# Routed expert blocks with two PSUM banks each for turned tokens and finished blocks, tokens turned two ahead, and lists built from 64 rows and 32 marks

## What is computed

```python
# E, F, K = 16 experts, 128 hidden units, 2 choices; 2 shared experts
y = gelu(x @ g[e] + gb[e]) * (x @ w1[e] + b1[e]);  out = y @ w2[e] + b2[e]
aff = sigmoid(x @ wa);  p, i = top_k(aff, 2);  p = p / sum(p)
routed = sum over the 2 chosen experts of p * expert(x)
shared = sum over the 2 shared experts of expert(x)
x = x + (x + shared + routed)     # on the layer-normed x within the brackets
```

## Time and profile before

| | us |
|---|---|
| median of 3 runs | 969.54 |
| lowest and highest | 968.85, 970.51 |
| the profiled execution, time of the run | 969.79 |
| the profiled execution, span in the profile | 968.5 |
| busy: PE, DVE, ACT, POOL | 879.2, 717.4, 596.9, 589.9 |
| layer 0: first `turn_in` to last `turn_out` | 604.21 to 667.47 |
| layer 1: first `turn_in` to last `turn_out` | 890.05 to 951.22 |

### The profile page before, as it was taken

How to read it: one execution, slowest core, us unless ns; L and a number is a source line. 1 busy time by engine, 2 the same in 40 slices (tenths; PEclk the granted TensorE clock), 3 DMA queues, 4 the chain that set the end, 5 groups by cost and what they waited for, 6 DMA issues and landing times.

```text
span 968.5 us, 23186 instructions
## 1 busy us (share of the span) xinstructions
PE 879.2 (91%) x9330; PEld 731.1 (75%) x9330; DVE 717.4 (74%) x1287; ACT 596.9 (62%) x970; POOL 589.9 (61%) x603
## 2 busy tenths in 40 slices
PE   8799999999999999999999898899689888888992
PEld 6578788878888888888788886788566447676981
DVE  4788889788888987897888758643594877357744
ACT  4888877787787687777876541453497345241551
POOL 4895698678677876886786844423338641332342
PEclk9999999999999999999999999999899899899997
DMA  4321212021112111121110393963012112462644
GB/s 124 112 76 65 73 45 88 34 77 56 65 56 78 45 67 56 45 88 34 44 56 2 96 259 115 312 230 132 11 44 68 22 30 55 131 172 94 237 153 164
DMA packets 68417, 89.79 MB, mean 93 GB/s; under 512 B 11570, under 2 KB 49494, under 8 KB 68310
## 3 DMA queue, kind: packets, MB, share of 16 engines
q1 hardware_dynamic: 63062, 77.81, 25.1%
q0 software_dynamic: 3072, 8.39, 2.8%
q10 hardware_dynamic: 2176, 2.10, 0.6%
HBM read 59.57 MB, written 8.52 MB: 70 GB/s over the span
## 4 chain that ended last, share of the span: by engine, by line
PE 57%; DVE 24%; POOL 5%; ACT 5%; issue 5%; DMA 2%; another core or an unknown queue 0%; ACTq 0%; DVEq 0%; POOLq 0%; SPq 0%
PE psum L826 21%; DVE arena L1945 7%; PE psum L1125 5%; PE psum L798 5%; PE psum L909 4%; PE psum L901 4%; PE psum L954 3%; PE psum L1139 2%; DVE arena L1982 2%; PE psum L1263 1%; DVE v L2378 1%; PE psum L1297 1%; PE psum L1227 1%; DVE arena L2001 1%; DMA arena<-scratch_y 1%
## 5 line engine op out<-in xcount | busy, mean ns | idle before, releaser
L826 PE MATMUL psum<-vT,split 128*128 128x512 f32 x1368 | 343.1, 400 | 7.9 <-DVE arena L1945 5.5
L1945 DVE SCALAR_TENSOR_TENSOR arena<-psum,arena 128x1023 f32<-128x1023 f32 (+2 forms) x208 | 265.7, 1278 | 74.0 <-ACT arena L1454 51.4
L826 PEld LDWEIGHTS psum<-vT,split 128*128 128x128 f32 x1368 | 248.8, 188 | 63.6 <-DVE arena L1945 7.6
L1454 ACT ACTIVATE arena<-psum,arena 128x512 f32<-128x512 f32 x160 | 109.1, 690 | 66.2 <-PE psum L826 65.6
L1471 ACT ACTIVATE arena<-arena 128x1024 f32<-128x1024 f32 x80 | 84.2, 1058 | 34.9 <-POOL arena L2557 23.3
L2530 POOL TENSOR_TENSOR split<-arena,split 128x256 fp32r<-128x256 f32 x114 | 83.6, 742 | 30.7 <-ACT split L1381 30.6
L2557 POOL TENSOR_TENSOR arena<-arena,v 128x1021 f32<-128x1021 f32 x32 | 76.3, 2386 | 41.8 <-DVE arena L1945 41.8
L798 PE MATMUL psum<-ident,arena 128*128 128x128 f32 x568 | 73.0, 274 | 9.8 <-POOL arena L2587 6.1
L798 PEld LDWEIGHTS psum<-ident,arena 128*128 128x128 f32 x568 | 63.9, 140 | 21.3 <-POOL arena L2587 9.7
L1125 PE MATMUL psum<-arena,vT 128*128 x496 | 67.0, 278 | 3.4 <-issue 1.9
L1125 PEld LDWEIGHTS psum<-arena,vT 128*128 128x128 f32 x496 | 60.3, 192 | 6.5 <-issue 6.3
(11 more groups left out here) (283 smaller groups left out, 1733.9 us busy)
## 6 DMA issues: line engine op xcount, KB each, us to landing
bcast<-scratch_a SPq DMA_DIRECT2D x32, 512.0 KB, 3.7
vT<-arena SPq DMA_DIRECT2D x62, 256.0 KB
arena<-in_w_a SPq DMA_DIRECT2D x16, 768.0 KB, 4.2
arena<-in_wout_a SPq DMA_DIRECT2D x8, 256.0 KB, 2.6
scratch_v<-v SPq DMA_DIRECT2D x8, 256.0 KB, 5.2
arena<-scratch_y ACTq DMA_DIRECT2D x8, 256.0 KB, 5.2
arena<-scratch_y SPq DMA_DIRECT2D x8, 256.0 KB, 5.3
arena<-in_wg SPq DMA_DIRECT2D x4, 512.0 KB, 5.9
```

Of the source, the lines that this page charges most:

```text
L826: m = pe.matmul(bank, split[:, t % SPLITS, i, q, :], vT[:, j, q, half * BANK:(half + 1) * BANK], start=(n == 0), stop=(n == 3 * KD - 1))
L1454: act.activation(tile[:, hs], wide_of(t)[:, hs], ACT.Identity, scale=w[:, TAPS - 1:TAPS], bias=0.0).then_inc(sem["tap0"], 1)
L1945: dve.scalar_tensor_tensor(out=tile[:, s:T], in0=bank[:, 0:T - s], scalar=cw_a[:, j, i, TAPS - 1 - s:TAPS - s], in1=tile[:, s:T], op0=ALU. ...
```

## The change

`in_bank` becomes two banks (2 and 4) and `out_bank` two (1 and 5), used in turn. `turn_in(i)` waits for `block_in(i - 2)` and `block_down(j)` for `block_out(j - 2)`. Banks 4 and 5 hold shared sums, so `turn_in(1)` waits for `add_shared(0)` and `block_down(1)` for `add_shared(1)`; these two move from steps 5 and 6 to before the first blocks on DVE, ahead of `add_v` of the same tokens. `turned_after(j)` is j + 2 for all j, with `turn_in(1)` ahead of `block_up(0)`. In a step PE does `block_down(j - 1)` before `turn_out(j - 17)`, and DVE `block_in(j + 2)` before `block_hidden(j)`.

The list's base is now a multiple of 64 (`SUB`): 32 marks to a list, 64 rows, a table `halves` for the 32 bases, one DVE instruction for all of `hot`, and 32 matmuls in `members` that give 64 partitions each. `members` stands ahead of both parts of `up(3)`.

```diff
 def turned_after(j):
-    return [1] if j == 0 else [2, 3] if j == 1 else [j + 2] if j + 2 < DENSE else []
+    return [j + 2] if j + 2 < DENSE else []
...
-ADD_SHARED_AT = (5, 6, 7, 8)
+ADD_SHARED_AT = (None, None, 7, 8)
...
-        out_bank, in_bank, row_bank = (psum[:, i * BANK:i * BANK + D] for i in (1, 2, 2))
+        out_banks, in_banks = ([psum[:, i * BANK:i * BANK + D] for i in pair] for pair in ((1, 5), (2, 4)))
+        row_bank = psum[:, 2 * BANK:2 * BANK + D]
...
 # members, PE
-                    for i in range(LISTS):
-                        on.wait_ge(sem["router"], n_router(n, f"hot{i // NC}"))
-                        m = pe.matmul(list_bank, hot[:, i, :], mark[:, i, :], start=(i == 0), stop=(i == LISTS - 1),
-                                      skip_group_check=True)
+                    on.wait_ge(sem["router"], n_router(n, "hot"))
+                    for h in range(P // SUB):
+                        for i in range(LISTS):
+                            m = pe.matmul(list_bank[h * SUB:(h + 1) * SUB, :], hot[:, i, :],
+                                          mark[:, i, h * DENSE:(h + 1) * DENSE], start=(i == 0), stop=(i == LISTS - 1),
+                                          skip_group_check=True)
...
 # turn_in, PE
-                    on.wait_ge(sem["blk_ht"], done + i)
+                    if i == 1:
+                        on.wait_ge(sem["x_sh"], NC // 2 * n + 1)
+                    if i >= 2:
+                        on.wait_ge(sem["blk_ht"], done + i - 1)
...
 # block_down, PE
-                    if j >= 1:
-                        on.wait_ge(sem["blk_y"], done + j)
+                    if j == 1:
+                        on.wait_ge(sem["x_sh"], NC // 2 * n + 2)
+                    if j >= 2:
+                        on.wait_ge(sem["blk_y"], done + j - 1)
...
                 up(2)
-                up(3, (0,))
                 members()
-                up(3, (1,))
+                up(3)
                 down(2)
...
                             turn_in(0)
                             down(3, (0, 1))
+                            turn_in(1)
                         block_up(j, at[j % GROUPED])
...
+                    if 1 <= j <= BLOCKS:
+                        block_down(j - 1)
                     if j >= SETTLED + 2:
                         turn_out(j - SETTLED - 2)
-                    if 1 <= j <= BLOCKS:
-                        block_down(j - 1)
...
 # places, DVE
-                    dve.tensor_tensor(mark, spread(G_["base"], DENSE),
-                                      floors[:, 0:DENSE].unsqueeze(1).to_broadcast([P, LISTS, DENSE]),
+                    dve.tensor_tensor(mark, spread(G_["base"], P // SUB * DENSE),
+                                      halves[:, :].unsqueeze(1).to_broadcast([P, LISTS, P // SUB * DENSE]),
                                       ALU.is_equal).then_inc(sem["router"], 1)
...
-                    for i in range(LISTS):
-                        m = dve.tensor_scalar(hot[:, i, :], column[:, :], G_["row"][:, i:i + 1], None, ALU.is_equal)
-                        if i % NC == NC - 1:
-                            m.then_inc(sem["router"], 1)
+                    dve.tensor_tensor(hot, spread(G_["row"], SUB), column[:, :].unsqueeze(1).to_broadcast([P, LISTS, SUB]),
+                                      ALU.is_equal).then_inc(sem["router"], 1)
...
 # add_shared, DVE
-                    on.wait_ge(sem["down"], len(STEPS) * (n + 1))
-                    on.wait_ge(sem["res"], NC // 2 * n + q + 1)
+                    on.wait_ge(sem["down"], len(STEPS) * n + (2 if q < 2 else len(STEPS)))
+                    if q >= 2:
+                        on.wait_ge(sem["res"], NC // 2 * n + q + 1)
...
                 skips()
+                add_shared(0)
...
-                block_in(0)
                 for j in range(BLOCKS + 2):
-                    if j == 0:
-                        block_in(1)
...
                         weights_in(j, at[j % GROUPED])
-                        block_hidden(j)
-                    if j >= 1:
+                        if j == 0:
+                            block_in(0)
+                            add_shared(1)
+                            block_in(1)
                         for i in turned_after(j):
                             block_in(i)
+                        block_hidden(j)
```

37 lines of the change are left out of this document (22 added, 15 removed).

## The result

The changed kernel takes 966.84 us in the median, the kernel before beside it on the same chip 969.50. The ratio is 0.9971, with a 95% interval of 0.9959 to 0.9983: a gain of 1.7 to 4.0 us where 8.7 were forecast, and a time 0.3 us above the range. The profiled execution took 965.88 us, its span is 964.3; before the span was 968.5, so the two traces differ by 4.2.

The account below looks back on a forecast made before the run. It took PE in the expert blocks as bound by its own pace and waits for single banks. 969.8 less 10.7 for the blocks, plus 0.4 for lists and 1.6 for a clock fall, gave 961.1, stated as 961.0; range 957.0 to 966.5.

Parts of the forecast that it names:

- Entry: From turn_in(0) to block_up(2): 5.7 us after the change, gains of 1.7 in layer 0 and 1.5 in layer 1.
- Early steps: From block_up(2) to block_up(15): gains of 0.5 us in layer 0, where transfers hold it, and 0.9 in layer 1.
- The order effect that was to make all of it wrong: On DVE, block_in(j + 2) ahead of block_hidden(j): a late gather could cost as much as the second bank brings.
- Middle and late steps: From block_up(15) to block_up(30): 2.5 us gained per layer, 0.45 of it from block_down covering ACT's one stop.
- Tail: After block 30, to the last scatter: 0.55 us gained in each layer.
- The list stage: Making the lists ahead of the blocks: 0.2 us lost in each layer, plus 1.6 for one clock fall in up(3).
- The clock: PE's clock falls in up(3) in one of the two layers, costing about 1.6 us.
- late steps at 1.69: Rival: late steps in the blocks do not get faster; 964.5 us, chance 0.25 together with two other rivals.
- a low clock reach into the blocks: Rival: the clock falls in both layers and stays low into the first blocks; slower, 975.5 us, chance 0.03.
- Early sums that drag the entry: Rival: turn_in(1) and block_down(1) wait for shared sums, the entry gains nothing; 964.2 us, chance 0.25 with two others.
- rivals 1, 2 and 5: Late steps stay at 1.69, transfers hold early steps, or early sums drag the entry: 963.5 to 966.5 us, chance 0.25.
- a mixture of two rivals: Two of the rivals at once: 966.5 to 967.6 us, chance 0.04.

Follow-up runs that it names:

- the group without stops: Second group of follow-ups: the changed kernel and the kernel before, both rerun unchanged; ratio 0.9923, 959.44 us, the kernel before 965.77.
- hidden_first: The changed kernel with block_hidden(j) ahead of block_in(j + 2) on DVE again; ratio 0.9917 to the kernel before.
- turn_out_first: The changed kernel with turn_out ahead of block_down in a step again, both banks kept; ratio 0.9966 to the kernel before.
- one_out_bank: The changed kernel with bank 1 alone for block_down's finished blocks, new order and two banks for turned tokens kept; ratio 0.9981 to the kernel before.
- After: The changed kernel itself, with both the banks and the new list, as first measured; 966.84 us, ratio 0.9971 to the kernel before.
- members_between: The changed kernel with members put between the two parts of up(3), six matmuls each, new list kept; ratio 0.9909, 956.27 us.
- after_third: The changed kernel, unchanged, measured once more in a group where the kernel before took 970.03 us; ratio 0.9988.
- banks_only: The kernel before with the banks and the new order alone, old list kept; ratio 0.9888, 954.64 us when first run.
- Groups 1 and 5: Two groups of follow-up kernels, each run beside the kernel before on the same chip; the kernel before took 965.22 and 969.85 us.
- filler: The changed kernel with eight matmuls that nothing reads put on PE ahead of members; ratio 0.9902, 957.10 us.
- owners_first: The changed kernel with members between the two parts of up(3), and owners ahead of tokens on DVE; ratio 0.9914, 957.17 us.

## Why the prediction was wrong, point by point

The sum was 10.7 for the blocks, less 2.0 for the list stage. In the traces of the first measurement it was 7.8 less 3.6; in the group without stops 11.2 less 3.55. Two steps failed: the stops of ACT, taken as one in each layer that the new order covers in part, and the list stage, taken as nearly free. Against the sum the stops' stretches, from block 15 to the last scatter, are 4.1 short, the list stage 1.6; the entry gave 1.7 more.

- **Entry** (1.7 and 1.5): mechanism right, size too small: 2.6 and 2.3, and 1.9 in both layers without stops. The 0.75 put in for waits wasn't there: PE needs 4.86 in every kernel that has two banks for turned tokens and `members` ahead of `up(3)`, near the 4.95 worked out for its work alone. Part of it is no gain: the blocks start later, while the gathers start when they did. With the old list, or `members` between the parts of `up(3)`, the entry takes 5.4 to 6.5, around the 5.7 forecast; so the size was right for a list stage that loses nothing.
- **Early steps** (0.5 and 0.9): 0.3 and 0.6, and 1.0 and 1.5 without stops. The order effect that was to make all of it wrong, `block_in` ahead of `block_hidden`, is nothing: hidden_first.
- **Middle and late steps** (2.5 in each, 1.7 and 1.1 measured, 1.8 in both without stops): this is one of the two steps that failed, in "ACT stops once in each layer" and the 0.45 that it was to give back. 1.34 and 1.56 a step came as worked out, and turn_out_first and one_out_bank show that both the order and the bank were needed, as the text had it. But I read one stop from one trace as a property of the kernel that a deeper pipeline covers in part. After has one stop in layer 0 and three in layer 1. Against the profiles without stops, these steps lost 1.5 in each layer of the kernel before, and 1.65 and 2.2 in after: where +0.45 was put in, -0.1 and -0.65 came. In layer 1 PE waits 0.97 for the hidden tile at the first stop, 0.24 at the second, where it has lost time already, and 1.65 at the last one, which falls into the tail.
- **Tail** (0.55 each): -0.1 and -0.7, the stop at `gelu(30)` again; without stops 0.5 and 0.8.
- **The list stage** (0.2 in each layer and one fall of 1.6): the other step that failed. 2.7 and 0.9 were lost. "hot as one row of 1.1 to 1.4" with `marks` "beside" it was the error: they exclude each other, so the list's matmuls started at 597.0 instead of 596.2. The other 1.6 in layer 0 is the fall, foreseen at its place and its price: `up(3)` took 4.60 instead of 3.02. That `hidden(3)` would wait for PE in both layers was right, and members_between shows that the wait goes when six matmuls stand ahead of the list. One price for layer 0 is more than the runs give, though: its stage took 15.7 us where the clock fell ahead of `up(3)` (one_out_bank), 17.2 to 18.0 where it fell in it, and 19.1 in after_third; layer 1, with no fall, took 15.1 to 15.5 in all of them, where the old list took 14.5 to 14.6.
- **The clock**: one fall in the two list stages, as counted. That the clock between the layers might change by some microseconds from execution to execution was not in the sum; the single runs of one kernel lie up to 4 us to either side of their median, and it may hold part of the list's cost.
- **The rivals**: late steps at 1.69 did not come, nor did a low clock reach into the blocks. Early sums that drag the entry did not show. The time fell just above the band of rivals 1, 2 and 5, in that of a mixture of two rivals, and none of them was the reason. No rival had the stops in it.
- **The range** was too narrow for what one profile can't show: the kernel before alone moved by 4.8 us between groups. The gain was 0.1 to 0.3% where ACT stopped and 0.8% where it did not; the forecast 0.9% lies within the interval of the second only. That it does is partly luck: there the blocks gave 0.5 more than forecast and the list stage took 1.55 more, and the change of the clock between the layers was in neither.

The version that beats both is banks_only: 0.9888, 0.9915 and 0.9902 in three groups, 8 to 11 us under the kernel before.

## What to carry to other kernels

Two edits that each look good can hide each other: one half of this change was worth 10 us, and the other took back between 3 and 9. Before an instruction with two SBUF inputs is put on DVE beside POOL's, look at what both read; before work is moved ahead of other work on an engine, ask what filled the wait that now is empty. And a stop that appears once in one trace, with no releaser on the core, should stand in the range, none of it or several in every layer at full price, and not in the sum.

## What the runs showed of the hardware

- A DVE TENSOR_TENSOR of two SBUF inputs and a POOL TENSOR_TENSOR run one after the other: 1.05 to 1.23 us each alone, 2.1 for the second when they start within 0.04 us.
- ACT stopped for 1.2 to 2.1 us ahead of instructions whose inputs the trace shows as ready, mostly three blocks apart and often at the same blocks in two profiles of a kernel, in groups where the kernel before took 970 us, and never from block 15 on where it took 965.5. Groups 1 and 5, on one and the same chip, differ in this.
- In filler the clock fell ahead of the place that was filled: PE was idle for 1.93 us ahead of `rank`, 0.50 was granted in 594 to 596, and `up(2)` took 3.90 us for 12 matmuls that take 3.02. In one_out_bank, without filler, the same numbers are 1.92, 0.50 and 3.84.
- Where the clock falls moves with small edits: into `up(3)`, into the entry (0.50 in 606 to 608 of members_between), or nowhere between 590 and 614, as in owners_first. It moves from one execution to the next as well: `up(3)` took 4.60 in after and 5.43 in after_third, the same program.
